# Causal attention with the scores of two steps issued together and both weighings after them

## The reference

```python
scores = jnp.einsum('bqhd,bkhd->bhqk', Q, K) / math.sqrt(D_K)     # 8 batches, 16 heads of 16, 1024 tokens
scores = jnp.where(causal, scores, -jnp.inf)
attn = jax.nn.softmax(scores, axis=-1)
out = jnp.einsum('bhqk,bkhd->bqhd', attn, V).reshape(Bx, Sx, N_HEADS * D_K)
```

## Time and profile before

| what | value |
|---|---|
| median of 3 runs | 2843.88 us |
| the profiled execution's own time | 2843.33 us |
| its span, first to last instruction | 2841.6 us |
| mean granted TensorE clock | 0.948 |
| TensorE matmul / weight load | 87% / 41% of the span |
| VectorE / ScalarE / GpSimd | 78% / 62% / 20% of the span |

### The profile page before, as it was taken

One profiled execution on the slowest core, in us unless ns is written; L12 is line 12 of the kernel. 1 busy time (PEld: TensorE's weight loads), 2 busy tenths in 40 slices (PEclk: granted clock), 3 DMA queues, 4 the chain that ended last, 5 costly groups with the idle time before them and its releaser, 6 DMA issues. The chain is left out here.

```text
span 2841.6 us, 57152 instructions
## 1 busy us (share of the span) xinstructions
PE 2466.9 (87%) x15239; PEld 1168.1 (41%) x15239; DVE 2226.1 (78%) x5740; ACT 1769.7 (62%) x2700; POOL 561.2 (20%) x644
## 2 busy tenths in 40 slices
PE   5887999999999999668999988994999999995656
PEld 2442333333333333354666655552333333333544
DVE  6887899999999888386777767995666666666968
ACT  2452566666666666316777756883788778872446
POOL 1443112121212121230000000222222222222200
PEclk9996999999999999799999999997999999998879
DMA  5985353535454443450000002555866676754403
GB/s 182 282 277 119 76 111 75 111 80 106 84 102 87 98 85 71 121 143 1 0 0 0 0 0 82 185 183 174 162 145 142 143 144 143 142 119 143 120 0 118
DMA packets 224107, 309.46 MB, mean 109 GB/s; under 512 B 32417, under 2 KB 170353, under 8 KB 211953
## 3 DMA queue, kind: packets, MB, share of 16 engines
q1 hardware_dynamic: 223616, 307.47, 44.9%
q10 hardware_dynamic: 432, 1.31, 0.2%
HBM read 181.29 MB, written 126.88 MB: 108 GB/s over the span
## 5 line engine op out<-in xcount | busy, mean ns | idle before, releaser
L941 ACT ACTIVATE a_p<-psum 128x1024 f32<-128x1024 f32 (+1 forms) x640 | 567.4, 941 | 310.1 <-PE psum L1039 309.9
L941 ACT ACTIVATE b_p<-psum 128x512 f32<-128x512 f32 (+2 forms) x640 | 444.1, 749 | 148.4 <-PE psum L1039 145.3
L993 DVE CUSTOM_DVE_ANT_0 a_dump<-psum,a_bias 128x128 bf16<-128x128 f32 (+3 forms) x1024 | 447.6, 488 | 65.3 <-PE psum L1028 57.6
L991 DVE TENSOR_REDUCE a_peak<-psum 128x1 f32<-128x512 f32 x512 | 334.4, 687 | 24.4 <-PE psum L1028 21.3
L970 DVE COPY b_twin<-psum 128x512 f32<-128x512 f32 (+1 forms) x320 | 203.9, 637 | 168.0 <-PE psum L1039 164.7
L1039 PE MATMUL psum<-b_qs,b_ks 96*128 96x512 bf16 (+3 forms) x1536 | 307.9, 330 | 31.2 <-DMA b_vs<-values 31.2
L1055 PE MATMUL psum<-b_p,b_vs 128*32 128x512 f32 (+3 forms) x3072 | 314.6, 497 | 6.3 <-POOL b_p L913 6.2
L913 POOL TENSOR_SCALAR_AFFINE_SELECT a_p<-a_p 128x512 f32<-128x512 f32 x256 | 162.3, 634 | 760.3 <-ACT a_p L941 748.5
L1028 PE MATMUL psum<-a_ks,a_qs 96*128 96x128 bf16 (+2 forms) x1008 | 274.8, 333 | 29.4 <-DMA a_vs<-values 20.2
L913 POOL TENSOR_SCALAR_AFFINE_SELECT b_p<-b_p 128x512 f32<-128x512 f32 x256 | 159.4, 634 | 444.5 <-DVE b_p L973 433.3
L1039 PE MATMUL psum<-a_qs,a_ks 98*128 98x512 bf16 x1008 | 236.1, 330 | 9.2 <-DMA a_qs<-a_rows 3.7
(11 more groups left out here) (197 smaller groups left out, 3668.3 us busy)
## 6 DMA issues: line engine op xcount, KB each, us to landing
qk_parts<-l_parts SPq DMA_DIRECT2D x96, 256.0 KB, 3.1
qk_parts<-g_parts SPq DMA_DIRECT2D x96, 256.0 KB, 2.8
values<-l_vx SPq DMA_DIRECT2D x64, 256.0 KB, 3.3
sums<-a_osb SPq DMA_DIRECT2D x64, 256.0 KB, 2.2
m_num<-sums SPq DMA_DIRECT2D x64, 256.0 KB, 3.8
m_inv<-reciprocals SPq DMA_DIRECT2D x64, 256.0 KB, 4.5
values<-g_vx SPq DMA_DIRECT2D x64, 256.0 KB, 3.1
sums<-b_osb SPq DMA_DIRECT2D x64, 256.0 KB, 2.1
```

Source lines behind the costliest of these rows:

```text
L941: act.activation(p[s % SLOTS][:, 2 * k:2 * k + heads, cols], m.psum[:, at:at + heads, cols], ACT.Exp if softmax else ACT.Square, scale=z.D ...
L991: last = dve.tensor_reduce(dst, piece, AX.X, ALU.max)
L993: last = dve.tensor_tensor_reduce(dump[c % SRING][:, at:at + w], piece, bias[:, 512 - w:], 1.0, NEG, ALU.add, ALU.max, dst)
```

## The change

`MOST` now holds six numbers for each pair of steps. In the softmax pass `unit` goes by two steps: it deals maxima ahead of each of the four score pieces of steps s + 2 and s + 3, deals more, weighs step s, deals more, weighs step s + 1. The order of the chunks and their number (36) are unchanged; a pair is dealt 8, but the pairs of steps (2, 3) and (8, 9) are dealt 6. ScalarE's first copy of the output bank goes one step later, behind the exponentials of step 5. The linear pass keeps its order.

```diff
-    MOST = [(1, 1, 0) if s in LAST else (1, 2, 1) for s in range(STEPS)]
-    assert sum(map(sum, MOST)) == CH
+    MOST = [(1, 1, 1, 1, 0, 2) if s == LAST[0] else (2, 1, 1, 1, 1, 0) if s + 1 == LAST[1] else (2, 1, 1, 1, 3, 0)
+            for s in range(0, STEPS, 2)]
+    assert sum(map(sum, MOST)) == CH and AHEAD == 2
...
-                    if s == LAST[0]:
+                    if s == LAST[0] + softmax:
                         take_sums(n, 0)
...
-                dealt = 0
-                for s in range(STEPS):
+                for s in range(0, STEPS, 2 if softmax else 1):
                     t = s + AHEAD
                     there = t < STEPS or ahead
                     if t == STEPS and ahead:
                         operands(n + 1, (r + 1) % RING, rnd + (r + 1) // RING)
                     at = (n, r, t) if t < STEPS else (n + 1, (r + 1) % RING, t - STEPS)
-                    for k in range(3):
-                        if k == 2:
-                            weigh(n, r, s)
-                        elif there:
-                            scores(*at, k)
-                        some_maxima(dealt, MOST[s][k])
-                        dealt += MOST[s][k]
+                    if not softmax:
+                        for k in range(2):
+                            if there:
+                                scores(*at, k)
+                        weigh(n, r, s)
+                        continue
+                    for k in range(4):
+                        some_maxima(MOST[s // 2][k])
+                        if there:
+                            scores(at[0], at[1], at[2] + k // 2, k % 2)
+                    some_maxima(MOST[s // 2][4])
+                    weigh(n, r, s)
+                    some_maxima(MOST[s // 2][5])
+                    weigh(n, r, s + 1)
```

More of the change, by code:

```diff
@@ L1065, in unit, with some_maxima @@
             def unit(n, r, rnd, ahead, far):
-                def some_maxima(first, count):
-                    if not softmax:
-                        return
+                dealt = [0]
+                def some_maxima(count):
                     late = CH - 2 * EARLY
-                    for k in range(first, first + count):
+                    for k in range(dealt[0], dealt[0] + count):
                         if k < late and ahead:
@@ L1077, in some_maxima @@
                             maximum_scores(n + 2, (r + 2) % RING, k - late, k - late + 1)
-                dealt = 0
-                for s in range(STEPS):
+                    dealt[0] += count
+                for s in range(0, STEPS, 2 if softmax else 1):
                     t = s + AHEAD
```

## The result

The changed kernel takes 2920.26 us (median of 4 runs, 2914.71 to 2924.32) against 2843.57 before: a ratio of 1.0275, 95% interval [1.0255, 1.0295]. It is slower by 77 us, where the prediction said 82. The profiled execution spans 2922.6 us against 2841.6.

What follows compares the result with a forecast made beforehand. The prediction took TensorE to bound the kernel, VectorE close behind. Pair sums of 30.63 us against 28.12 gave 2.51 more in 30 units, 75 us, plus 8 for the last two: 2926 us, range 2875 to 2950.

Steps and rivals of the forecast that it cites:

- What the change saves: Where two weighings adjoin, in four of five pairs, TensorE saves 0.24 us: 0.96 us a unit, about 30 us.
- The wait for the exponentials: In each pair with wide steps, score pieces wait for ScalarE's exponentials, costing 0.65 us; only 0.2 for narrow step 2.
- VectorE's ring of three: Three banks hold VectorE 2.0 us of work; in a pair with 8 chunks the eighth waits, making 6.11 us.
- Pair B and the copy: Steps 2 and 3: output copy behind four exponentials holds step 3's weighing until 4.95, not 4.27; pair 6.17 us.
- The rows' delay in D: Steps 6 and 7: VectorE, having made the rows, is 0.87 us late; the pair takes 6.98 us.
- Transfers: Waits for operand load (1.3 us) and rows (0.3 to 0.5) go; load ready at 15.55, TensorE there at 16.0.
- The total: 30 units at 2.51 us more give 75 us, the last two units 8: 2926 us.
- neither bound binds: TensorE saves 0.96 us a unit, then runs into the load: period 27.6, 0.5 less, 2828 us; chance 0.11.
- the clock falls: TensorE's busy share falls to about 0.86; a tenth of the pass at half clock adds some 45 us, 2970; chance 0.06.

Runs made afterwards that it cites:

- the run with both edits: Changed kernel with two of the eight row DMAs issued by ScalarE and the values loaded under their own semaphore: 30.76 us a unit, ratio 1.0284.
- both transfer edits: Kernel before with two of the eight row DMAs issued by ScalarE and the values loaded under their own semaphore: ratio 0.9927.
- the rows on two queues: Kernel before with two of the eight row DMAs issued by ScalarE, beside SyncE's six: ratio 0.9956.
- half of both: Changed kernel with VectorE reducing half of each piece and ScalarE taking half of the exponentials: 27.67 us a unit, ratio 0.9949.

## Why the prediction was right, point by point

- *What the change saves*: shown. Joined weighings take 1.86 us and the entry, as worked out.
- *The wait for the exponentials*: shown to 0.01 us in the pairs, and by the run with half the exponentials, which gives 2.3 us a unit. The 0.35 that the early copy gives is inside these 2.3.
- *VectorE's ring of three*: shown by the run with half the maxima (1.65 us) and by the chunk between the weighings.
- *Pair B and the copy*: the stall is there (0.7 by the starts), and half of it is the move's. Undoing it gives 0.35, because the copy can't begin before 3.95 us; the other half (4.60 against the 4.27 at which TensorE would be there) is there with the copy at its old place too.
- *The rows' delay in D*: 7.09 against 6.98; VectorE comes to D's first chunk at 7.69 us instead of 7.53. No run takes the rows' making away.
- *Transfers*: the load wait and the row wait go, and the run with both edits shows that neither is close enough to matter. I had put the load 0.45 us ahead of TensorE. It was about 1.0: its last DMA is issued at 609.51 and such a one lands after 9.3 us, and TensorE comes at 619.82.
- *The total*: 75 + 8 us, measured 81 between the profiled executions and 77 between the medians. The terms are less exact than their sum. The steady units gave 30 x 2.64 = 79 rather than 75. The last two units gave 4 (29.31 to 30.34, and 17.38 to 20.25 to the end of the last weighing) rather than 8. And the units of before weren't all steady: 30 of them took 28.34 on average, not 28.12, which takes 6.6 off; 5.1 of it is in two units of 31.69 and 29.64 that ran in part at the lower clock. The rest, some 4.5 us, lies ahead of the first weighing (2.8) and behind the pass. So that the total came within 5 us owes something to luck.
- *Rival "neither bound binds"*: its period of 27.6 was measured at 27.67, when both bounds were removed (and with less work in it). But its reason for the kernel before, that the load decides it, was wrong: the load's wait can be taken away there without gain.
- *Rival "the clock falls"*: false up to the last two units, and there the other way round. From 270 to 1212 us the granted clock of the changed kernel is 1.00, with TensorE busy 88% and gaps of at most 0.63 us. Its last two units, where TensorE's gaps reach 1.93 us, hold 10.2 us at the lower level of 1.2 GHz, from 1214.5; the kernel before has 6.8 us in the same place, from 1138.5. Ahead of its last two units the kernel before had two such stretches, of 6.8 us from 312.5 and 3.4 from 961.0, right behind load waits of 2.20 and 1.50 us. Another wait, of 2.19 at 1047, had none behind it. The wait and the stretch at 961 (the last figures of the second row are clock, DMA share and GB/s):

```profile
960.95 0.60 PE L1028 MATMUL psum<-a_ks,a_qs 96*128 96x128 bf16 x2 [1.50 <-DMA a_vs<-values]
...
961.00:964.40 3.40, 3.40 (x15) 0.91 (x16) 1.68 (x9) 0.00 (x0) 0.36 (x1) 0.50 0.02 2
```

- The busy share of TensorE is 27.22 of 30.76, 0.88, where I had said 0.86.

## What to carry to other kernels

Before joining work to save a switching cost, walk one period with the depth of every buffer the other engines live on: how long each of them has nothing, and how long the first engine waits at the other end. Here 0.24 us a switch was bought with two steps' scores in a row on one pair of banks and with a ring of three that must bridge 1.95 us. And a wait seen in the profile, even 27 us of it, is not the bound until the next one behind it is known: it fell to zero once without any gain, and taking it away gained something only where the wait for the rows was gone too.

## What the runs showed that I had not expected

- A unit's period becomes exact when no transfer is late: 30.75 or 30.76 in all 30 of the changed kernel, 27.58 or 27.59 in 29 of 30 with both transfer edits, against 28.06 to 31.69 before.
- One copy of 128 x 512 moved by one place in ScalarE's queue cost 49 us in 2839.
- A late load can cost more than its wait. Between 270 and 1100 us there are eight stretches at half the granted clock: two in the kernel before, two with the rows on two queues, four with half of both. Each begins within 1.5 us behind a load wait of 1.5 to 2.4 us, and the other kernels, where no load is as late, have none. But most such waits in these three kernels are followed by no stretch, and no run was made to part the two.
